# Unit 6 of the T matrix made one stage later, and four changes of order, in a two-layer graph network on one core

## The reference

```python
h = relu(layernorm(x))
# layer 0: attention weights, then two propagations
Xw = h @ Wv + bv
e = leaky_relu(sj[None, :] + si[:, None] + ab, 0.2)      # sj, si: Xw @ halves of aw
alpha = adj * exp(e);  T = alpha / (sum(alpha, -1) + 1e-12)
H = h @ Wk[0] + bk[0] + (T @ h) @ Wk[1] + bk[1] + (T @ T @ h) @ Wk[2] + bk[2]
x = x + relu(H)
# layer 1: one normalized graph convolution
h = relu(layernorm(x));  A1 = adj + I;  dh = rsqrt(sum(A1, -1))
x = x + relu((dh * A1 * dh) @ h @ kernel + bias)
```

## Time and profile before

| | |
|---|---|
| median of 3 runs | 768.02 us (767.58 to 768.12) |
| profiled execution, its own time | 767.7 us |
| its span, first to last instruction | 765.9 us |
| busy PE / DVE / ACT / POOL | 747.6 / 615.1 / 536.4 / 188.9 us |
| mean granted clock of PE | 0.998 |

### The profile page before, as it was taken

The page is one execution under the profiler, slowest core; times in us unless marked ns, Lnnn a source line. Parts: engine busy times, 40 slices in busy tenths (PEclk is TensorE's granted clock), DMA queues, the critical chain, the costliest instruction groups (busy, mean ns, idle before and its releaser), DMA issues.

```text
span 765.9 us, 14033 instructions
## 1 busy us (share of the span) xinstructions
PE 747.6 (98%) x5099; PEld 686.4 (90%) x5099; DVE 615.1 (80%) x1417; ACT 536.4 (70%) x1044; POOL 188.9 (25%) x190
## 2 busy tenths in 40 slices
PE   8799999999999999999999999999999999999997
PEld 8598988999889897999979999799988999889986
DVE  7896888778897788877989678896888877885665
ACT  3897696567956689557885668856697567956351
POOL 3031150322303123040322214132150312302330
PEclk9999999999999999999999999999999999999999
DMA  7656458654486355872667625776348654455521
GB/s 226 214 206 222 147 159 299 192 194 148 154 304 215 117 164 176 270 244 84 193 204 266 220 95 179 250 232 221 102 160 291 187 206 139 163 172 178 169 67 55
DMA packets 63909, 143.32 MB, mean 187 GB/s; under 512 B 6768, under 2 KB 32864, under 8 KB 63840
## 3 DMA queue, kind: packets, MB, share of 16 engines
q1 hardware_dynamic: 55072, 111.75, 44.4%
q10 hardware_dynamic: 8768, 30.68, 11.6%
HBM read 133.96 MB, written 8.45 MB: 186 GB/s over the span
## 4 chain that ended last, share of the span: by engine, by line
PE 56%; DVE 17%; ACT 14%; issue 5%; POOL 4%; DMA 3%; ACTq 0%; SPq 0%; DVEq 0%
PE da L1042 13%; PE acc L1174 8%; PE acc L1176 8%; PE acc L1175 8%; PE db L1042 7%; ACT tg_e L523 4%; ACT tmp L459 3%; PE tp L1140 3%; PE tp L1142 3%; PE tp L1141 3%; DVE t_lo L809 3%; ACT tg_e L529 3%; POOL hs_lo L404 2%; DVE p L835 2%; DVE p L840 2%
## 5 line engine op out<-in xcount | busy, mean ns | idle before, releaser
L1174 PE MATMUL acc<-g_hi,t_hi 128*128 128x256 f32 (+1 forms) x1024 | 291.1, 284 | 3.2 <-DVE g_lo L778 2.8
L1176 PE MATMUL acc<-g_hi,t_lo 128*128 128x256 f32 (+1 forms) x1024 | 289.4, 283 | 0.0
L1175 PE MATMUL acc<-g_lo,t_hi 128*128 128x256 f32 x1024 | 288.8, 282 | 0.0
L1174 PEld LDWEIGHTS acc<-g_hi,t_hi 128*128 128x128 f32 x1024 | 193.5, 189 | 4.4 <-issue 3.2
L1175 PEld LDWEIGHTS acc<-g_lo,t_hi 128*128 128x128 f32 x1024 | 194.2, 190 | 0.3
L1176 PEld LDWEIGHTS acc<-g_hi,t_lo 128*128 128x128 f32 x1024 | 194.0, 189 | 0.0
L398 POOL TENSOR_TENSOR g_lo<-tmp,g_hi 128x256 fp32r<-128x256 f32 x64 | 63.9, 999 | 269.2 <-ACT g_hi L578 269.2
L815 DVE TENSOR_TENSOR a_lo<-a_raw,a_hi 128x512 fp32r<-128x512 f32 x128 | 89.8, 721 | 25.1 <-ACT a_hi L566 25.0
L523 ACT ACTIVATE tg_e<-si,sij 128x256 f32<-128x256 f32 x256 | 109.2, 499 | 0.3 <-DMA si<-si_rows_dram 0.2
L566 ACT CAST a_hi<-a_raw 128x512 fp32r<-128x512 f32 x128 | 75.8, 615 | 20.7 <-DVE a_raw L854 14.8
L578 ACT CAST g_hi<-tmp 128x256 fp32r<-128x256 f32 x64 | 25.8, 404 | 84.0 <-DVE tmp L829 83.8
(11 more groups left out here) (147 smaller groups left out, 1537.7 us busy)
## 6 DMA issues: line engine op xcount, KB each, us to landing
a_raw<-adj_dram SPq DMA_DIRECT2D x64, 512.0 KB, 4.5
a_raw<-adj_z_dram SPq DMA_DIRECT2D x64, 512.0 KB, 4.4
tg_a<-adj_t_dram ACTq DMA_DIRECT2D x58, 512.0 KB, 4.2
x_o<-x_dram SPq DMA_DIRECT2D x64, 128.0 KB, 3.4
out_dram<-x_o SPq DMA_DIRECT2D x64, 128.0 KB, 3.6
x_nat<-x_dram SPq DMA_DIRECT2D x28, 256.0 KB, 4.1
xt<-x_t_dram SPq DMA_DIRECT2D x28, 256.0 KB, 4.3
si<-mean_rows_dram SPq DMA_DIRECT2D x7, 512.0 KB, 4.9
```

What stands on the lines that cost most here:

```text
L1174: nc.tensor.matmul(acc[:, s, 0:n], l_hi, r_hi, start=(jt == 0), stop=False)
L1175: nc.tensor.matmul(acc[:, s, 0:D], l_hi, r_lo, start=False, stop=False)
L1176: ins = nc.tensor.matmul(acc[:, s, 0:n], l_lo, r_hi, start=False, stop=(jt == NT - 1))
```

## The change

Unit 6 of samples 1 to 7 no longer is made in Z of the sample before (steps 9, 10, 11, 14, 15 of Z) but in U of its own sample, one tile ahead of unit 7: `leaky` and `exponent` of unit 6 in tile 0 and of unit 7 in tile 1 (before: 7 in tile 0), `t_prod` 6 in tile 1 and 7 in tile 2, `t_high` in tiles 2 and 3, `t_low` in tiles 3 and 4. The load that each `t_high` issues moves with it. Four changes of order stand beside it: (a) in Z, `t_prod` of unit 5 goes from step 6 to step 8, behind zt_low; (b) in Z, hs_high of the last two tiles goes from step 1 to step 2, behind the cast a_hi(3,0); (c) in sample 0, ACT copies the mean rows before it begins unit 6 instead of in tile 2 of U; (d) in sample 0, PE awaits g2 column tile by column tile inside row tile 0 instead of all of it ahead.

```diff
-    LEAKY_Z, EXP_Z = {5: 5, 9: 6}, {6: 5, 10: 6}
-    HIGH_Z, HIGH_U = {0: 3, 5: 4, 11: 5, 14: 6}, {2: 7}
-    PROD_Z, PROD_U = {1: 4, 6: 5, 11: 6}, {1: 7}
-    LOW_Z, LOW_U = {3: 3, 7: 4, 12: 5, 15: 6}, {3: 7}
+    LEAKY_Z, EXP_Z = {5: 5}, {6: 5}
+    HIGH_Z, HIGH_U = {0: 3, 5: 4, 11: 5}, {2: 6, 3: 7}
+    PROD_Z, PROD_U = {1: 4, 8: 5}, {1: 6, 2: 7}
+    LOW_Z, LOW_U = {3: 3, 7: 4, 12: 5}, {3: 6, 4: 7}
...
-                    if i == (2 if b == 0 else 3) and not last:
+                    if i == 3 and b > 0 and not last:
                         mean_copy(b + 1)
...
-                    if i == 0:
-                        leaky(b, NU - 1)
-                        exponent(b, NU - 1)
+                    for u in ({0: (NU - 1,)} if b == 0 else {0: (NU - 2,), 1: (NU - 1,)}).get(i, ()):
+                        leaky(b, u)
+                        exponent(b, u)
...
-                    if q == 1:
+                    if q == 2:
                         hs_high(b, par, NG - 1)
...
             for u in range(HJ, NU - 1):
+                if u == NU - 2:
+                    mean_copy(1)
                 leaky(0, u)
...
-                pe.wait_ge(g2_ready, b * NT + NT)
+                if b > 0:
+                    pe.wait_ge(g2_ready, b * NT + NT)
...
-                    accumulate(b, U_PHASE, i, g1_tmp_ready, v_tmp_done, None, D + 2,
+                    accumulate(b, U_PHASE, i, g1_tmp_ready, v_tmp_done, g2_ready if b == 0 else None, D + 2,
```

## The result

The changed kernel takes 769.16 us, median of 11 executions (767.97 to 769.95), and the kernel before, on the same chip, 767.56 (median of 11, 765.84 to 768.88). The ratio is 1.002, with a 95% interval of 1.0012 to 1.0029: slower by 0.2%, and a ratio of 1 lies outside the interval. The forecast was 766.0, faster. The time lies in the range and is that of the rival with three collisions, 769.2, but the likeliest case was another, and on the other side.

What follows compares the result with a forecast made beforehand. PE was taken as the bound, busy 747.6 of 765.9 us. Beginning -0.45, layer 1 -4.4 and propagation +2.6 gave -2.25; set against the 768.0 median and rounded, with a little for DMA collision: 766.0, range 763.2 to 770.0.

Steps and rivals of the forecast that it cites:

- the rival with three collisions: Propagation (U): three POOL collisions make unit 7 late, 0.94 us in each of six samples; 769.2 us, chance 0.20.
- the likeliest case: Whole kernel: two collisions in the propagation and the clock falling before the first dense part; 766.0 us, chance 0.34.
- In tiles 3 and 4 ACT is free in time: Propagation: prompt ACT casts bring POOL collisions in tiles 3 and 4, 0.55 us each; tile 2 is nearly a tie.
- I take two collisions: 2.6 us: Propagation: t_lo(7) ends 0.31 us late for row tile 6, costing PE 0.4 us in six samples, 0.2 in sample 7.
- Layer 1: Z: later unit 5 product and hs_high shorten PE's waits for zt_lo and a_lo; about 0.63 us per sample, 4.4 us gained.
- They stand behind step 8 there, where PE waits for nothing, so that is worth 0: Z: taking unit 6's leaky, exponent, cast and two DVE passes out of layer 1 gains 0.
- about 0.23 stays: Z, piece 6: of the 0.86 us lost to a_lo in three samples, about 0.23 remains after moving hs_high.
- The waits before tiles 2 and 4: Sample 0's beginning: PE stands about 2.0 us before tile 2 and 2.9 before tile 4, which starts at 51.25 as before.
- I take the fall: gain 0.45: Sample 0's beginning: removing the ht_lo wait gains 1.95 us, a clock fall behind tile 4 costs 1.5; gain 0.45.
- The mean rows behind two loads: Propagation: 512 KB more loads close ahead of the mean rows' DMAs could delay the dense part; taken as 0, at most 0.5 a sample.

Runs made afterwards that it cites:

- the passes first: The changed kernel, but in U of samples 1 to 7 DVE makes each tile's t_prod or t_low before its output chunk; 761.68 us, ratio 0.9922, lowest median of all versions.

## Why the prediction came out wrong

**The step that failed** is "In tiles 3 and 4 ACT is free in time; in tile 2, with two leakys and exponents ahead, POOL and DVE arrive within 0.1 us of one another", and with it "I take two collisions: 2.6 us". The mechanism was right: POOL getting in ahead of DVE's pass, 0.55 us each, deadline at tile 6. Its count was not. In tile 2 too POOL was there first, 326.25 against 326.50, and by 0.25 in every one of samples 1 to 6. The leaky and exponent of unit 7 didn't make ACT late: in sample 3 DVE's tmp is done at 325.72, and ACT begins the cast of g1_hi at 325.76. The term was 7.4 instead of 2.6. The rival with three collisions had the wait right: unit 7 0.86 late, and the rows show 0.90 of idle. But both cases counted too little behind the wait, the rival 0.08. PE lost 1.17 for its 0.90 of idle; the 0.2 to 0.3 more that a stop costs beside its idle time, which I had added in layer 1, I added only in part here. With one collision less it is the same: 0.38 idle, 0.65 lost. That this rival's 769.2 is the measured median is partly luck: its propagation was 1.6 too low (5.8 against 7.4), and its layer 1 gave 0.9 too little (4.4 against 5.3). In tile 1 there was no collision, as forecast.

**Layer 1** gave 5.3 in the profile against 4.4, so the sum was near, and the reasons only half right. "They stand behind step 8 there, where PE waits for nothing, so that is worth 0" is wrong: with the four orders alone, the product of unit 6 makes PE wait 0.53 for output chunk 0's bank, and the gain of layer 1 is gone. A place where PE waits for nothing now isn't free once PE comes there 0.7 us earlier. Also "about 0.23 stays" at piece 6 was too careful: nothing stays in any sample of the changed kernel. The race itself isn't gone, though: in the profiles of the passes first and of unit 6's product one step later a wait of 0.57 for a_lo stands once, in sample 0, and Z lasts 26.40 and 26.43 there.

**The beginning.** The waits before tiles 2 and 4 stand as forecast (1.94, and 2.4 to 2.5 in the profiles in which no slow stretch precedes it; forecast 2.0 and 2.9), the mean copy at 45.09 instead of "about 44.5", and the dense part doesn't wait for ht_lo. "I take the fall: gain 0.45" has the fall where four of six profiles show it, but its reference was one execution of the kernel before whose wait was the longest of those seen. In the executions of the three kernels with (c), (d) or both no gain can be told.

**The mean rows behind two loads**, taken as 0 in samples 1 to 6, are 0 in the changed kernel: no wait for ht_lo there. With unit 6's product one step later, where t_lo isn't late, two such waits appear (0.46 and 0.43), so the reason given, that DVE's lateness gives the rows time, fits; the fastest version, with unit 6 in U and no lateness, has none, so it isn't shown to be the whole reason.

**The medians.** The profiles differ by 0.3, the medians by 1.6. The changed kernel's 11 times reach from 767.97 to 769.95 without a clear gap, and the profiled one, in which the slow stretch is hidden, is the lowest of all. That most of the others had it on the path would fit the 1.5 us that the two places differ by in the profiles, but it isn't shown: only one execution of each kernel has a trace. It can't be the whole of it either, since one of the 11 took 768.77 at a mean granted clock of 1.0, where the profiles with a slow stretch in the beginning have 0.997 or 0.998.

Set right, the sum against the profile is -2.0 - 5.3 + 7.4 = +0.1 with the slow stretch hidden, and about +1.6 with it on the path; measured +0.3 in the profile, +1.6 in the medians.

The Trainium skill (GPSIMD Engine Reference, section Specifications) says that contention with VectorE comes with instructions that read two SBUF inputs. The traces agree, in both directions: passes with two SBUF inputs were lengthened by 0.55, the output chunk's first instruction, which reads PSUM, was not (0.48). What decided the sign was who waits, and how often, and that is read from the rows of these runs.

The slow stretch began at 43.49 in the changed kernel and at 52.17 with both changes of the beginning alone, behind the same two waits of one program up to there. The Trainium skill (TensorE: Matmul & The Clock Gate, Part 1) says that the number of slow matmuls at a kernel's start varies from run to run of the same kernel. The traces agree in kind only: here it is a stretch in the middle of the run whose place varies.

## What to carry to other kernels

Where two engines contend, count the collisions from the order of instructions, not from arrival times a tenth apart: put the long two-input pass ahead of the short ones, with an instruction behind it that reads at most one SBUF input, so that the partner arrives inside it and waits, rather than at its edge, where it gets in ahead of the next two-input pass; here that order alone was worth the 7.4 us of the propagation. When a wait is removed, list the next deadlines behind it and move all that are closer than what you gain, for each fix alone may show nothing. And take the cost of a wait that hangs on a DMA from several executions; one profile showed 1.73 where others showed 0.6 to 0.7.

## What the runs showed of the hardware

- DVE and POOL don't share by halves. A running pass isn't interrupted in these traces: DVE's 1.22 stayed 1.22 while POOL's subtraction waited inside it (0.74 alone, 1.21 then). At the boundary of two DVE passes with two SBUF inputs each, POOL is let in, and the second pass shows 1.76 or 1.77, 19 times in propagations 1 to 7 of the changed kernel.
- Behind the two waits of the new beginning, the first of 1.7 to 2.0 us and the second of 2.4 to 2.5 (1.1 and 1.3 where the stretch came before it), the granted clock fell to 0.50 once in each profile, for 3.4 us, in two behind the first (43.49, 44.01) and in four behind the second (52.28, 52.17, 51.76, 51.76). With g2 alone, waits of 1.71 and 2.50, it didn't fall at all. Behind the old wait of 2.8 it fell in four of six profiles; in one of the other two it fell later, behind a wait of 2.30, and in one not at all. So an idle of that length isn't always followed by it.
- The same broadcast of the mean rows, issued at 56.59 in the kernel before and at 56.81 in that with hs_high later, let DVE go on at 62.00 and at 61.18, 5.4 and 4.4 us later, with both programs the same up to there.
